# Side slices of a transformer block placed on every second tile of a half batch

## What is computed

```python
scores = clip(einsum('bhqd,bhkd->bhqk', qh, kh) * scale)
decay = exp(-LAMBDA_DECAY * TIME_STEP * abs(idx[:, None] - idx[None, :]))
attn = softmax(clip(scores * decay), axis=-1)
out = einsum('bhqk,bhkd->bhqd', attn, vh) @ Wo
x = layernorm(x + out)
x = layernorm(x + moe_out(x) + shared(x))
```

## Time and profile before

| | |
|---|---|
| median of 3 runs | 689.81 us (685.57 to 691.2) |
| the profiled execution | 684.16 us |
| its span, first to last instruction | 682.4 us |
| TensorE busy | 649.8 us, 95% |
| ScalarE busy | 550.2 us, 81% |
| the 512 exponentials of 128x1024 | 480.1 us busy, 1044 ns each |
| VectorE, GpSimd busy | 308.6 us, 275.9 us |
| mean granted TensorE clock | 0.991 |

### The profile page before, as it was taken

One profiled execution on the slowest core, in us unless ns is written; L12 is line 12 of the kernel. 1 busy time (PEld: TensorE's weight loads), 2 busy tenths in 40 slices (PEclk: granted clock), 3 DMA queues, 4 the chain that ended last, 5 costly groups with the idle time before them and its releaser, 6 DMA issues.

```text
span 682.4 us, 12888 instructions
## 1 busy us (share of the span) xinstructions
PE 649.8 (95%) x4763; PEld 290.6 (43%) x4763; DVE 308.6 (45%) x993; ACT 550.2 (81%) x645; POOL 275.9 (40%) x259
## 2 busy tenths in 40 slices
PE   8999999999999999999999999999999997999992
PEld 4223333333333343333333333333335986775651
DVE  5434333453444345543434452435443442375793
ACT  5788999999999999999999999999996442342252
POOL 3965505603430551145044445503551105537621
PEclk9999999999999999999999999999999999899997
DMA  5658993572472256237425493333354788732121
GB/s 164 216 186 308 389 332 128 185 264 93 152 241 102 93 201 223 98 121 253 173 93 198 132 297 128 131 121 111 115 179 147 219 261 240 237 96 74 36 64 49
DMA packets 73540, 116.83 MB, mean 171 GB/s; under 512 B 6592, under 2 KB 49152, under 8 KB 73472
## 3 DMA queue, kind: packets, MB, share of 16 engines
q1 hardware_dynamic: 54944, 102.06, 44.3%
q10 hardware_dynamic: 15456, 7.59, 3.8%
q0 software_dynamic: 3072, 6.30, 3.3%
HBM read 68.73 MB, written 48.76 MB: 172 GB/s over the span
## 4 chain that ended last, share of the span: by engine, by line
PE 78%; DVE 5%; DMA 5%; ACT 5%; issue 2%; POOL 2%; SPq 1%; ACTq 0%; DVEq 0%; POOLq 0%
PE ps L977 29%; PE ps L961 19%; PE ps L1111 7%; PE ps L899 4%; PE ps L1106 4%; ACT probs L815 4%; DMA keys<-stack_dram 3%; PE ps L1120 2%; PE ps L1122 1%; PE ps L996 1%; PE ps L1031 1%; PE ps L1026 1%; DVE ps L1435 1%; PE ps L1028 1%; PE ps L1124 1%
## 5 line engine op out<-in xcount | busy, mean ns | idle before, releaser
L815 ACT ACTIVATE probs<-ps 128x1024 f32<-128x1024 f32 x512 | 480.1, 1044 | 19.6 <-DVE ps L1435 12.1
L977 PE MATMUL ps<-probs,V 128*18 128x512 f32 x2048 | 269.5, 598 | 0.5 <-ACT probs L815 0.4
L961 PE MATMUL ps<-queries,keys 32*128 32x512 f32 (+3 forms) x1408 | 181.1, 408 | 5.6 <-DMA keys<-stack_dram 3.7
L1435 DVE TENSOR_TENSOR ps<-ps,cpk 128x256 f32<-128x256 f32 x256 | 102.1, 429 | 126.9 <-PE ps L961 111.1
L961 PEld LDWEIGHTS ps<-queries,keys 32*128 32x128 f32 x1408 | 92.4, 182 | 148.8 <-ACT probs L815 87.2
L602 POOL TENSOR_TENSOR stage<-qk,rows_sb 128x512 fp32r<-128x512 f32 x32 | 40.9, 1278 | 121.0 <-DVE qk L1282 116.2
L644 POOL DMA_INDIRECT sorted_dram<-xn,slots x48 | 47.1, 982 | 61.7 <-ACT probs L815 49.4
L865 ACT ACTIVATE probs<-ps 128x512 f32<-128x512 f32 x48 | 28.5, 596 | 53.2 <-PE ps L1111 23.2
L1111 PE MATMUL ps<-xnT,stage 128*128 128x512 f32 x128 | 58.9, 593 | 0.0
L977 PEld LDWEIGHTS ps<-probs,V 128*18 128x18 f32 x2048 | 34.4, 96 | 55.7 <-issue 40.6
L1557 DVE TENSOR_TENSOR probs<-probs,ps 128x512 f32<-128x512 f32 x48 | 32.7, 687 | 51.0 <-PE ps L1106 15.0
(11 more groups left out here) (192 smaller groups left out, 588.5 us busy)
## 6 DMA issues: line engine op xcount, KB each, us to landing
stack_dram<-stage SPq DMA_DIRECT2D x60, 512.0 KB, 6.6
keys<-stack_dram SPq DMA_DIRECT2D x30, 512.0 KB
queries<-stack_dram SPq DMA_DIRECT2D x30, 512.0 KB
keys<-stack_dram SPq DMA_DIRECT2D x30, 256.0 KB
keys<-expert_dram SPq DMA_DIRECT2D x28, 192.0 KB
sorted_dram<-y_pre SPq DMA_DIRECT2D x1, 4096.0 KB, 18.6
rows_sb<-expert_dram SPq DMA_DIRECT2D x16, 192.0 KB
V<-expert_dram SPq DMA_DIRECT2D x16, 192.0 KB
```

What stands on the lines that cost most here:

```text
L815: nc.scalar.activation(probs[:, m % 3, 2 * j:2 * j + 2, :], ps[:, 2 * s:2 * s + 2, :], ACT.Exp, scale=SCALE).then_inc(exp_done, 1)
L961: last = mm(bank[2 * s + i][:, lo:hi], keys[rows, u, kt // CT, v, tok(kt % CT)], queries[rows, u, v, lo:hi], start=True, stop=True)
L977: last = mm(bank[OUT_BANK][32 * i:32 * i + 2 * (HD + 1), :], V[:, c // 2 % 2, kt, k + i, half * (HD + 1):(half + 2) * (HD + 1)], probs[:, ...
L1435: tt(d, d, diag_fix.unsqueeze(1).to_broadcast([P, 2, P]), ALU.mult).then_inc(diag_done, 1)
```

## The change

The table of the half batches 0 to 6 gets one form instead of two (the last half batch keeps its own). In half batches 1 to 5 there are 16 slices, one at every second tile from 0 to 30, where there were 20 (odd) or 23 (even). `xT`, `o`, `a`, `x`, `lg`, `norm` and `cnt` are now whole, `q`, `k`, `wo` and `v` in two parts. Half batch 0 overrides most entries; there only `o` of half batch 0 (tiles 20 and 21 become 22) and `norm` of half batch 2 (27 and 28 become 28) differ. In half batch 6 the results for `p` fall away, and the flag moves from tile 14 to 10.

```diff
-            elif c % 2:
-                places = {("xT", p): (0,), ("o", 2 * d + 1): (1,), ("q", p): (4, 5, 6), ("a", d): (7, 8), ("k", p): (9,),
-                          ("wo", d): (13, 14), ("v", p): (15, 16), ("o", 2 * c): (19, 20), ("x", d): (22,),
-                          ("lg", d): (23, 24), ("norm", p): (26, 27), ("cnt", d): (29,)}
             else:
-                places = {("o", 2 * d + 1): (1, 2), ("xT", p): (3, 4), ("q", p): (5,), ("a", d): (7, 8), ("k", p): (10, 11),
-                          ("wo", d): (12, 13), ("v", p): (16, 17, 18, 19), ("o", 2 * c): (20, 21), ("x", d): (23, 24),
-                          ("lg", d): (26,), ("norm", p): (27, 28), ("cnt", d): (30,)}
+                places = {("xT", p): (0,), ("o", 2 * d + 1): (2,), ("q", p): (4, 6), ("a", d): (8,), ("k", p): (10, 12),
+                          ("wo", d): (14, 16), ("v", p): (18, 20), ("o", 2 * c): (22,), ("x", d): (24,),
+                          ("lg", d): (26,), ("norm", p): (28,), ("cnt", d): (30,)}
...
             if c == NCH - 2:
-                places["flag", 0] = (14,)
+                places["flag", 0] = (10,)
```

## The result

The changed kernel took 700.2 us (median of 4 runs, 697.09 to 703.29), the kernel before 690.5 us in the runs beside it; the ratio is 1.0173, with a 95% interval of 1.0123 to 1.0224. Slower, by about what was forecast (701 us). The profiled execution took 700.75 us with a span of 698.9, 16.6 us over the profiled one of before.

What follows compares the result with a forecast made beforehand. ScalarE's exponentials were taken as the bound, 58.7 us per half batch plus lateness, on which alone the change acts. Terms 5.4 + 1.1 + 1.5 + 0.7 + 1.7 + 0.5 = 10.9, rounded to 11, on 689.8 gave 701 us; range 693 to 708.

Steps and rivals of the forecast that it cites:

- The price: Slices ahead of crossing tiles cost their length less 0.1 us at most, since the correction takes the room.
- Odd half batches: Half batches 1, 3, 5: slices ahead of crossing tiles and VectorE's terms cost 5.2 for 3.4 us, +1.8 each, +5.4.
- `norm` with `choose`: Odd half batches, VectorE: keeping `norm` and `choose` now follow each other in one round, costing 0.83 us.
- The keeping of `v`: Odd half batches, VectorE: this step moves from a plain into a crossing round, costing 0.20 us.
- Even half batches: Half batches 2 and 4: slices ahead of crossing tiles, `lg`, `cnt` and keeping `wo` make 4.9 us; +1.1 and +1.5.
- the order steps: Half batch 4: ordering steps of the first three half batches come a round later, +0.7 us (0 to 1.2).
- Half batch 6: No work for `p`; slices, `lg`, `cnt` and `wo` cost 3.8 in the place of 2.1 us, +1.7.
- Half batch 0: `o` whole ahead of a crossing tile costs +0.5 us; `norm` ahead of a plain one, nothing.
- The loads: Rival: loads come late at half batch starts, five borders pay, +6 us, 707 us; chance 0.14.
- TensorE's total: Rival: TensorE's total work is the bound, only slice lengths count, 3.6 us less, 686 us; chance 0.06.
- absorption: Rival: two rounds' free 0.84 us absorb every slice but `lg`, -8 us in even half batches, 682 us; chance 0.06.
- Costs little: Rival: a delay once paid stays as reserve over an empty round, half of the 11 us, some 695; chance 0.12.

Runs made afterwards that it cites:

- The pairs: Changed kernel with the parts of `k` at tiles 10 and 11 and of `v` at 18 and 19 in odd half batches; 700.18 us.
- the kernels without corrections: Kernel before and changed kernel, both with the diagonal's correction left out (part of the computation missing); 676.43 us with the old table, 685.86 with the new.
- `wo` put early: Changed kernel with `k` at tiles 10 and 11 and `wo` at 12 and 13 in even half batches; 698.9 us.
- second profile: Changed kernel run again without an edit, beside the same runs of the kernel before; ratio 1.0255 (1.0181 to 1.0329).
- fewer slices at the old places: Kernel before with results of two transposes each in neighbouring tiles put whole at the first tile, 18 and 19 slices for 20 and 23; 687.5 us.
- the kernel mended in both: Changed kernel, odd half batches: `k` at 10, 11, `wo` at 13, 14, `norm` at 23; even: `k` at 10, 11, `wo` at 12, 13; ratio 1.0129.

## Why the prediction was right

The forecast, 701 us against 700.2, rested on one step (that it came so near is partly luck, see the end of this section): slices with an empty round between them each pay in full ahead of a crossing tile, because the correction has taken the room. The pairs and the kernels without corrections show this step by itself.

Its terms:

- **The price** was 0.49 to 0.54 for a slice of 0.59 to 0.64 and measured 0.48 to 0.59; `lg` 0.89 and 0.88. I left out the small change, some 0.06 at slices called free, 0.2 to 0.3 us in a half batch.
- **Odd half batches** were forecast at +1.8, and 3 measured +2.4, 5 +2.7: in 3 `norm` cost 0.22 and not 0.1, and the load 0.39 and not nothing; `norm` with `choose` cost 0.72 of 0.83. The keeping of `v` cost 0.1 in one odd half batch and 0.37 in the others, for 0.20; I did not look into the difference. Half batch 1 measured only +1.4, because the profiled execution of before had lost 1.0 us there to a wait for keys and the changed one had not; without its tile 0 it grew by 2.4.
- **Even half batches**: +1.1 and +2.2 (with the order steps) measured +1.0 and +2.3. For half batch 2 this is luck of the same kind: before, it had lost 0.7 us to keys at tile 0, and without tile 0 it grew by 1.6. In both an error was made good by another: `cnt` cost nothing at tile 0 of half batch 4, since the stall at tile 31 had paid for it (0.43 as soon as that was gone), and the empty rounds' small change took its place.
- **Half batch 6** was +1.7 and measured +2.0 when the clock held, +4.3 when it didn't.
- **Half batch 0**: +0.5, measured +1.0. `o` cost its 0.48, but `norm` of half batch 1 stands one round behind it (tile 23), and TensorE could not begin it until VectorE, behind the corrections of tile 24, had emptied the side bank: 0.68 at tile 25 in the place of 0.14. I had put this at nothing.

**The loads** were the rival with 0.14, and it was half right. I had said that those in even half batches just fit. At the starts of 3 and 5 they came 0.4 us late, 0.8 us in all, shown by `wo` put early. What I did not see is that a load's own time varies between executions by more than its slack: for half batch 2 the last part took 5.04 us in the first profile and 6.01 in the second, where ScalarE lost 1.3 us. For half batch 4 the keys came 2.3 us later after the start of half batch 3 than before the change, and TensorE 2.6 us later, so no slack grew, and of the 0.5 us that the pairs won in half batch 3, 0.3 were given back at the next start.

One of the two signs that were to show the prediction wrong, a wait of TensorE of over 1 us for keys at a half batch's start, appeared in the second profile (1.19 us). It was a poor sign: the kernel before has two such waits in its own profile, 1.5 us ahead of half batch 1 and 1.1 ahead of 2. The other sign, no stall at 10, 12, 18 and 20 of an odd half batch, did not appear.

**TensorE's total** and **absorption** are refuted by fewer slices at the old places and by the stalls that each spaced slice ahead of a crossing tile showed. The 78% of the chain was no proof of a bound: it only said which engine stood between two exponentials. **Costs little** is refuted by the pairs: no reserve is carried over an empty round.

How near the number came is partly luck. The profiled execution of the changed kernel added 16.6 us where 10.9 were forecast for it; some 2.3 us of half batch 6 and 1.8 behind the last exponential are not the table's own, which leaves over 12. Between the medians lay 9.7 us in the first comparison and 16.8 in the second. What stays open is how much of this is clock and load in a usual execution.

## What to carry to other kernels

Where a pipeline has a fixed depth, as here, the price of inserted work depends on the latency of the tile behind it, not on the mean room: read it at each kind of place. Evenly spaced inserts are best ahead of places with room (no stall in 56 exponentials) and bad ahead of places without, where the second of two neighbours pays 0.27 us and one spaced apart 0.58. And before moving a step for its slot, follow what hangs on it (here statistics, parts, store, load) to the next start: a gain that ends at a load is no gain.

## What I had not expected of the hardware

TensorE's granted clock fell to its lower level, 1.2 GHz (0.50 in the rows), in the middle of the attention, here from about 410 to 416 us in the changed kernel. The stretches around this fall, at the start of half batch 6:

```profile
406.00:408.00 2.00, 1.90 (x16) 1.02 (x16) 0.56 (x3) 1.88 (x2) 0.97 (x1) 1.00 0.41 123
408.00:410.00 2.00, 1.66 (x16) 0.80 (x8) 1.67 (x8) 1.64 (x3) 0.00 (x0) 0.87 0.98 342
410.00:412.00 2.00, 2.00 (x10) 0.16 (x8) 0.43 (x1) 2.00 (x3) 0.87 (x1) 0.50 0.95 314
...
414.00:416.00 2.00, 2.00 (x20) 0.67 (x16) 0.27 (x1) 1.48 (x2) 0.00 (x0) 0.50 1.15 335
```

It cost some 2.2 us there: the stalls at tiles 2 and 3 were 1.45 and 0.89, and in the second profile, whose clock held, 0.14 and none. In the kernel without corrections and the new table the fall came right behind a wait for keys in which TensorE was busy for 0.46 of 2 us:

```profile
275.00:277.00 2.00, 0.46 (x8) 0.22 (x10) 0.76 (x4) 0.02 (x1) 0.00 (x0) 0.99 1.05 336
277.00:279.00 2.00, 2.00 (x16) 0.32 (x16) 0.00 (x0) 1.86 (x2) 0.00 (x0) 0.50 1.00 395
```

In the second profile of the changed kernel it fell at the start of half batch 2, in the wait of 1.19 us for keys. There the wait cost 1.3 us and the slower tiles 1 and 2 behind it 1.9: half batch 2 took 3.1 us more than in the first profile.

The fall shown first had no such wait ahead of it. The keys of half batch 6 had landed 1.1 us before TensorE issued its scores, and TensorE's pause, 0.34 us, was for an exponential. And not each wait for keys brought a fall: the profiled execution of before waited 1.5 and 1.1 us for them at the starts of half batches 1 and 2 and kept its clock. The Trainium skill ("TensorE: Matmul & The Clock Gate", HAM oscillation) tells of such falls in kernels whose TensorE pauses while it waits for loads. The falls in the wait of 1.19 us and behind that of 2.19 agree with it; the page speaks of longer pauses than the 0.34, 1.19 and 2.19 us seen here, and here these rows decide. What brings a fall in this kernel stays open: one in half batch 6 of the kernel mended in both came at tile 28 (467.9 us), with no wait for a load.
